# Raw expert projections drawn in the drains of two sixteen-head attentions, and GpSimd's gate products held until the routing is chosen

## The chip, the cores and the metric

One NeuronCore of a Trainium2 chip. The metric is the device time of one execution of the program in microseconds (us), median of several runs. Engines are named as in the profile: PE is TensorE's matmul, PEld its weight load, DVE VectorE, ACT ScalarE, POOL GpSimd, SP the engine that issues DMAs.

## What is computed

A stack of four layers over 16 sequences of 128 tokens of width 128 (2048 tokens in all). Each layer adds a gated cross-attention and a gated feed-forward to the residual stream `x`. The change concerns the last two layers:

```
x = x + tanh(g_xattn[2]) * L2_xattn(layernorm(x), ctx, ctx, mask)      # stage a2, 16 heads of 8
x = x + tanh(g_ffn[2])   * L2_ffn(layernorm(x))                        # stage f2
x = x + tanh(g_xattn[3]) * L3_xattn(layernorm(x), ctx, ctx, mask)      # stage a3, 16 heads of 8
x = x + tanh(g_ffn[3])   * L3_ffn(layernorm(x))                        # stage f3

L2_ffn: p = softmax(x @ gate); keep the top 2 of 8 experts
        y = sum_e p_e * silu(x @ W_e + b_e);  out = y @ combine
L3_ffn: s = sigmoid(x @ gate), 32 experts in 8 groups; best 4 groups, then best 6 experts, renormalised, * 2.5
        y = sum_e c_e * ((silu(x @ g_e) * (x @ u_e)) @ d_e) + one shared expert of the same form
```

## The kernel before

All data stay in SBUF; `x` is held token-major (16 blocks of 128 tokens), `xnt` is the layernormed stream, feature-major. Every stage is one Python function that returns five generator programs, one per engine. `in_turn` strings the stages together on each engine: a program yields twice, and the part ahead of its first yield is placed inside the last part of the stage before it, ahead of what that stage still has to do behind its own second yield. So each engine has one instruction list in a fixed order, with semaphore waits between engines, and nothing is reordered when it runs.

**Attention (`small_head_attention`, a2 and a3).** For each of the 16 blocks, PE makes the scores in banks 0 to 3 of PSUM (L872, L879), DVE takes maxima (L1124) and subtracts them (L1131), ACT takes the exponential (L1049), PE transposes (L893), ACT copies to SBUF (L1072), PE gathers the values (L906), and the result of a block is turned to tokens (L921), normalised on DVE (L1110, L1114), turned back (L930), copied by ACT (L1061), multiplied with `wo` (L937), and added to `x` on DVE (L1100) with its statistics (L1103, L1105). POOL makes the reciprocal roots for pairs of blocks (L325 to L332), ACT scales a pair (L341), PE turns it (L363) and ACT keeps it in `xnt` (L370). The *drain* is what is left after the last block's subtraction: two more blocks' turn-back, `out`, residual, and the last three pairs of blocks. There banks 0 to 3 are free, and PE, ACT and DVE wait for one another in a chain.

**Feed-forward (`feed_forward`, f2 and f3).** The tokens go in NG = 4 groups of 512; with J tiles (experts) there are N = 4 J steps: 32 in f2, 68 in f3. An *up* is the projection of one group with one expert: one 128x512 matmul in f2, a gate (L1788) and a second one (L1781) in f3; in fp32 the profile counts each as two instructions. ACT applies the function and writes to a ring of 512-column slots (L1885); in f3 ACT also copies the second projection (L1891) to one of two slots `u` and POOL multiplies the two (L2019). The routing: `logits` (L1526) for groups 0 to 2 before the first yield and for group 3 after it, a copy by ACT (L1559), a transpose (L1533), then the *choice*, a long chain of small DVE operations (`Route.choose`), then for each group a turn back on PE (L1547, semaphore `parts`) and a copy to `combt` by ACT (L1574). PE's loop over steps m does the up of step m + `ahead`, the selector matmul that spreads the weight of step m (L1809), and the *down* of step m - LAG (L1834; in f2 L1821, for two tiles that POOL has added, L2026). DVE multiplies with the weight (L1965). `ahead` ups are thus done before the choice ends: 12 in f2, 16 in f3. Of these, B = 3 (f2) and 2 (f3) lie ahead of the first yield, so ACT's functions for them stand ahead of its last scale (L341) and keep (L370) of the attention. In f3, from step 8 on, selector weights come by DMA (`spread`) instead of PE.

At the end of a group DVE adds to `x` (L1972) and takes statistics; in f2 POOL makes the root four steps later (L2039 to L2047), ACT scales (L1899) and PE turns (L1844).

`feed_forward` already has `early` and `given`: the first layer's attention a0 lets PE write the first raw projections of f0 (`early_up`) and DVE copy them unchanged from PSUM to the ring (`put_by`, L1799); ACT takes the function in place later (`take_function`). f2, a3 and f3 do without: their `early` is 0.

## Time and profile before

| | us |
|---|---|
| median of 3 runs | 1172.62 (1172.36 to 1173.94) |
| the profiled execution, its own time | 1173.72 |
| its span in the profile | 1172.0 |
| PE busy | 1093.0 (93%) |
| DVE busy | 725.7 (62%) |
| ACT busy | 702.9 (60%) |
| POOL busy | 469.0 (40%) |
| mean granted TensorE clock, share of 2.4 GHz | 0.978 |

The profiled execution is 1.1 us above the median, and 1.7 us of its time lie outside the span. PE is busy nearly everywhere, so what matters is where it is not: the page's forty slices show two tenths of idle PE in the slices of the two drains (slices 27 and 34 of 40, 29.3 us each), and the granted clock below 1 there.

### The profile page before, as it was taken

How to read it: one execution, taken by the hardware profiler on the slowest of the kernel's cores; microseconds unless marked ns; L12 is line 12 of the kernel's file. 1: busy time of each engine (PE TensorE's matmuls, PEld its weight loads, DVE VectorE, ACT ScalarE, POOL GpSimd, SP SyncE). 2: the span in 40 equal slices, each digit the busy share in tenths (PEclk: the TensorE clock that was granted, in tenths of full speed). 3: DMA queues.
4: the chain of work that ended last, by engine and by line, in shares of the span. 5: the costliest groups of instructions: out<-in, count | busy, mean ns of one | idle time of the engine just before them, and what ended most of it. 6: DMA issues, size and time to landing. Idle time of an engine off the chain costs nothing. (4 is left out here: it accounts for less than half of the span.)

```text
span 1172.0 us, 22896 instructions
## 1 busy us (share of the span) xinstructions
PE 1093.0 (93%) x8937; PEld 788.4 (67%) x8937; DVE 725.7 (62%) x1399; ACT 702.9 (60%) x1288; POOL 469.0 (40%) x741
## 2 busy tenths in 40 slices
PE   5998998899999999999997989988979988999998
PEld 3553478788888888888886646653646663466667
DVE  6775666565556656566654259974659994555554
ACT  4674711566665666666665568876458986644440
POOL 5772002223332233443344364431574634544440
PEclk9899999899999999999999999999989998999999
DMA  9200001000000000000000200000000000032220
GB/s 347 83 2 1 1 1 66 8 1 2 1 1 2 1 2 2 1 1 2 1 1 1 55 1 2 2 2 1 1 1 2 1 2 1 10 106 100 99 72 19
DMA packets 13884, 29.42 MB, mean 25 GB/s; under 512 B 2737, under 2 KB 5073, under 8 KB 13010
## 3 DMA queue, kind: packets, MB, share of 16 engines
q1 hardware_dynamic: 13778, 27.96, 6.9%
q8 instruction: 72, 1.18, 0.4%
q14 instruction: 34, 0.28, 0.1%
HBM read 25.14 MB, written 1.25 MB: 23 GB/s over the span
## 5 line engine op out<-in xcount | busy, mean ns | idle before, releaser
L1347 POOL TENSOR_TENSOR work<-work 128x1024 f32<-128x1024 f32 x64 | 121.3, 1896 | 268.2 <-DVE work L1441 268.2
L1428 DVE TENSOR_REDUCE work<-psum 128x8 f32<-128x1024 f32 x64 | 78.0, 1219 | 86.3 <-PE psum L1227 86.3
L1369 ACT ACTIVATE work<-work 128x1024 f32<-128x1024 f32 x64 | 67.4, 1053 | 95.8 <-DVE work L1432 95.8
L1439 DVE TENSOR_REDUCE work<-work 128x8 f32<-128x1024 f32 x64 | 77.4, 1209 | 71.7 <-ACT work L1369 71.7
L1834 PEld LDWEIGHTS psum<-w_down,work 128*128 128x128 f32 x768 | 99.2, 191 | 26.2 <-issue 24.3
L1834 PE MATMUL psum<-w_down,work 128*128 128x128 f32 x768 | 100.6, 275 | 0.9 <-DVE x L1972 0.7
L1124 DVE TENSOR_REDUCE work<-psum 128x8 f32<-128x1024 f32 x64 | 75.4, 1219 | 23.9 <-PE psum L879 23.6
L1072 ACT ACTIVATE work<-psum 128x512 f32<-128x512 f32 x128 | 74.2, 597 | 21.4 <-PE psum L893 20.7
L893 PEld LDWEIGHTS psum<-ident,work 128*128 128x128 f32 x512 | 57.2, 142 | 40.6 <-issue 21.7
L1432 DVE TENSOR_TENSOR work<-psum,work 128x1024 f32<-128x1024 f32 x64 | 78.4, 1225 | 6.7 <-DVE work L1428 0.5
L893 PE MATMUL psum<-ident,work 128*128 128x128 f32 x512 | 76.3, 280 | 5.4 <-ACT work L1072 3.6
L1227 PEld LDWEIGHTS psum<-work 64*128 64x128 f32 x1024 | 59.6, 188 | 24.4 <-issue 23.5
L1131 DVE TENSOR_TENSOR work<-psum,work 128x1024 f32<-128x1024 f32 x64 | 75.0, 1213 | 0.0
L1373 ACT ACTIVATE work<-psum 128x512 f32<-128x512 f32 x128 | 69.1, 596 | 2.3 <-PE psum L1242 2.3
L1242 PE MATMUL psum<-ident,work 128*128 128x128 f32 x512 | 66.4, 273 | 1.3 <-ACT work L1373 1.3
L1049 ACT ACTIVATE work<-work 128x1024 f32<-128x1024 f32 x64 | 67.2, 1053 | 0.2
L1788 PE MATMUL psum<-xnt,ctx_tok 128*128 128x512 f32 x128 | 66.7, 603 | 0.0
L1227 PE MATMUL psum<-work 64*128 64x128 f32 x1024 | 65.8, 278 | 0.7 <-ACT work L1364 0.7
L1781 PE MATMUL psum<-xnt,big 128*128 128x512 f32 x128 | 65.7, 594 | 0.0
L1259 PE MATMUL psum<-work 128*64 128x128 f32 x1024 | 63.0, 276 | 0.0
L1242 PEld LDWEIGHTS psum<-ident,work 128*128 128x128 f32 x512 | 57.9, 141 | 1.7 <-issue 1.7
L2019 POOL TENSOR_TENSOR big<-big,work 128x512 f32<-128x512 f32 x32 | 41.0, 1280 | 44.5 <-ACT work L1891 44.5
(351 smaller groups left out, 2447.5 us busy)
## 6 DMA issues: line engine op xcount, KB each, us to landing
work<-chosen SPq DMA_DIRECT2D x80, 128.0 KB, 3.0
x<-in_x SPq DMA_DIRECT2D x2, 512.0 KB, 4.8
ctx_tok<-in_ctx SPq DMA_DIRECT2D x2, 512.0 KB, 6.3
xnt<-in_xt SPq DMA_DIRECT2D x1, 1024.0 KB, 8.8
ctxt<-in_ctxt SPq DMA_DIRECT2D x1, 1024.0 KB, 10.6
mask<-in_mask SPq DMA_DIRECT2D x1, 1024.0 KB, 9.4
w_down<-in_down SPq DMA_DIRECT2D x1, 1024.0 KB, 7.9
ctx_tok<-in_g SPq DMA_DIRECT2D x1, 1024.0 KB, 4.7
```

What stands on the lines that cost most here:

```text
L893: mm = pe.transpose(bank[4 + g % 2][:, i * P:(i + 1) * P], prob[:, b % 2, h * P:(h + 1) * P], k.ident[:, :])
L1072: act.activation(probt[:, g, :], bank[4 + g % 2][:, :], ACT.Copy).then_inc(S["pt"], 1)
L1124: dve.tensor_reduce(nmax[:, b % 2, 8 * half:8 * half + 8], s, AX.X, ALU.max, negate=True)\
L1131: dve.tensor_tensor(prob[:, b % 2, half * 1024:(half + 1) * 1024] .rearrange("p (h c) -> p h c", c=P), s, nmax[:, b % 2, 8 * half:8 * half ...
L1227: mm = pe.matmul(bank[2 * half + r][:, c * P:(c + 1) * P], qt[rows, u % 2, at:at + P], kt[rows, u % 2, at:at + P], start=True, stop=True)
L1242: mm = pe.transpose(bank[4 + t % 2][:, n * P:(n + 1) * P], prob[:, u % 2, 8 * half + 4 * r + c % 4, :], k.ident[:, :])
L1347: pool.tensor_tensor(prob[:, u % 2, h, :], prob[:, u % 2, h, :], rinv[:, u % 2, h].unsqueeze(2).broadcast_to([P, 8, P]), ALU.mult)\
L1373: act.activation(probt[:, t, :], bank[4 + t % 2][:, :], ACT.Copy).then_inc(S["pt"], 1)
L1428: dve.tensor_reduce(nmax[:, u % 2, h], s, AX.X, ALU.max, negate=True).then_inc(S["max"], 1)
L1432: dve.tensor_tensor(prob[:, u % 2, h, :], s, nmax[:, u % 2, h].unsqueeze(2).broadcast_to([P, 8, P]), ALU.add)\
L1439: dve.tensor_reduce(rsum[:, u % 2, h], prob[:, u % 2, h, :], AX.X, ALU.add).then_inc(S["sum"], 1)
L1834: mm = pe.matmul(y[g % 2][:, b * P:(b + 1) * P], h[:, b * P:(b + 1) * P], tiles[j][4], start=j == 0 and b == 0, stop=j == J - 1, skip_grou ...
```

## The change

Both attentions get the number of the next stage and the number of raw pieces it wants. In the drain PE writes the first three pieces (`early_up`), DVE copies them out between its own steps (`put_by`), and the rest (4 in f2, 5 in f3) come from the next stage's part ahead of its first yield. A piece is one 128x512 projection: f2 takes 7 pieces, which are 7 tiles, f3 takes 8, which are 4 tiles. ACT takes the functions of f3's four tiles at once after the router's scores; f2's seven are spread over its later steps, one per step where f0 had two. `ahead` of f2 goes from 12 to 15, with a longer ring in weights that are no longer needed (wv1, wo1). In f3 the two slots `u` become sixteen, fourteen of them in dead weights, and POOL waits for `parts`, the end of the choice, before its first product. DVE's set-up of a3's key mask, which stood behind f2's choice, now stands ahead of it. Lines of the changed file are 1 to 12 higher than before (L893 is L894, L1788 is L1800, L1885 is L1897, L2019 is L2029).

```diff
@@ small_head_attention, tensor
                 turn(b - 1, 0)
                 if b >= 3:
                     turn_back(b - 3)
+                if b == NB:
+                    pe.wait_ge(S["sub"], 2 * NB)
+                    k.made[next_stage].early_up(pe, 0)
...
+        k.made[next_stage].early_up(pe, 1)
         turn_back(NB - 2)
         out(NB - 2)
         turn_to_tokens(NB - 1)
         after.turn(pe, NB // 2 - 3)
+        k.made[next_stage].early_up(pe, 2)
         turn_back(NB - 1)
@@ small_head_attention, vector
+        k.made[next_stage].put_by(dve, 0)
         residual_of(NB - 3)
         normalise_of(NB - 2)
+        k.made[next_stage].put_by(dve, 1)
         residual_of(NB - 2)
         normalise_of(NB - 1)
+        k.made[next_stage].put_by(dve, 2)
         residual_of(NB - 1)
+        for piece in range(3, pieces):
+            k.made[next_stage].put_by(dve, piece)
@@ feed_forward
-    u = a.take(2 * GT, "p (n c) -> p n c", n=2) if second else None
+    u = [*u_slots, a.take(GT), a.take(GT)] if second else ()
+    U = len(u)
...
-    ring = [one[:, n * GT:(n + 1) * GT] for one in spare for n in range(NG)][:R]
+    ring = [*(one[:, n * GT:(n + 1) * GT] for one in spare for n in range(NG)), *extra][:R]
@@ scalar
-                if n >= early + 2:
-                    act.wait_ge(S["prod"], n - 1)
-                act.activation(u[:, n % 2, :], bank[2 + n % 2][:, :], ACT.Copy).then_inc(S["second"], 1)
+                if n >= U:
+                    act.wait_ge(S["prod"], n - U + 1)
+                act.activation(u[n % U], bank[2 + n % 2][:, :], ACT.Copy).then_inc(S["second"], 1)
...
         for m in range(N + LAG + TURN + 1):
-            for of in (next(functions, None), next(functions, None)):
-                if of is not None:
-                    take_function(of)
             if m + ahead < N:
                 activate(m + ahead)
             if routed and 1 <= m < len(r.turns):
                 r.keep(act, m)
+            if (of := next(functions, None)) is not None:
+                take_function(of)
@@ vector
         yield
+        yield
         if routed:
             r.choose(dve)
         for m in range(N + LAG + TURN + 1):
-            if m == mask_at:
-                yield
@@ gpsimd
         if second:
+            pool.wait_ge(r.S["parts"], 1)
             for n in range(N):
                 multiply(n)
@@ build
-            return feed_forward(k, prev, "f2", 5, up2, ACT.Silu, ahead=12, lags=(4, 7, 8), on_act=True, one_down=True,
-                                spare=(k.big[0], k.big[2], k.negb),
+            return feed_forward(k, prev, "f2", 5, up2, ACT.Silu, ahead=15, lags=(4, 7, 8), on_act=True, one_down=True,
+                                early=7, given=3, extra=halves("wv1", "wo1"), spare=(k.big[0], k.big[2], k.negb),
...
-            return feed_forward(k, prev, "f3", 7, up3, ACT.Silu, ahead=16, lags=(0, 0, 0),
+            return feed_forward(k, prev, "f3", 7, up3, ACT.Silu, ahead=16, lags=(0, 0, 0), early=4, given=3,
+                                u_slots=halves("wq1", "wk1", "wv1", "wo1", "up0", "down0", "wfc", "wproj"),
```

How instructions move. First, PE at the end of a3 before, from the gather of the last block to the last turn of the attention (L363) and f3's first projection (L1788):

```order
L906 MATMUL psum<-work 32x128 x16
L930 MATMUL psum<-ident,work 128x128
L937 MATMUL psum<-w_wo,work 128x128
L921 MATMUL psum<-ident,work 128x128 x2
L363 MATMUL psum<-ident,work 128x128 x2
L930 MATMUL psum<-ident,work 128x128
L937 MATMUL psum<-w_wo,work 128x128
L363 MATMUL psum<-ident,work 128x128 x2
L1526 MATMUL psum<-xnt,w_gate 32x512 x3
L1788 MATMUL psum<-xnt,ctx_tok 128x512
```

and the same place in the changed kernel (numbers are one or a dozen higher):

```order
L907 MATMUL psum<-work 32x128 x16
L1793 MATMUL psum<-xnt,big 128x512
L931 MATMUL psum<-ident,work 128x128
L938 MATMUL psum<-w_wo,work 128x128
L922 MATMUL psum<-ident,work 128x128 x2
L363 MATMUL psum<-ident,work 128x128 x2
L1800 MATMUL psum<-xnt,ctx_tok 128x512
L931 MATMUL psum<-ident,work 128x128
L938 MATMUL psum<-w_wo,work 128x128
L363 MATMUL psum<-ident,work 128x128 x2
L1537 MATMUL psum<-xnt,w_gate 32x512 x3
L1793 MATMUL psum<-xnt,big 128x512
```

Two projections now stand between the drain's small steps (a third, not shown, a little ahead), and five instead of four behind the router's three logits. Second, ACT at the start of f3 before, from its second-last keep (L370) of a3's pairs:

```order
L370 ACTIVATE xnt<-psum 128x256
L1885 ACT_TABLE_LOAD
L1885 ACTIVATE big<-psum 128x512
L1891 ACTIVATE work<-psum 128x512
L1885 ACTIVATE big<-psum 128x512
L1891 ACTIVATE work<-psum 128x512
L341 ACTIVATE work<-x,rstd 128x128 x2
L370 ACTIVATE xnt<-psum 128x256
L1559 ACT_TABLE_LOAD
L1559 ACTIVATE work<-psum 128x512
L1885 ACT_TABLE_LOAD
L1885 ACTIVATE big<-psum 128x512
```

and now:

```order
L370 ACTIVATE xnt<-psum 128x256
L1565 ACT_TABLE_LOAD
L1565 ACTIVATE probe<-floor 128x1
L341 ACTIVATE work<-x,rstd 128x128 x2
L370 ACTIVATE xnt<-psum 128x256
L1570 ACTIVATE work<-psum 128x512
L1918 ACT_TABLE_LOAD
L1918 ACTIVATE big<-big 128x512 x4
L1897 ACTIVATE big<-psum 128x512
L1903 ACTIVATE w_wv<-psum 128x512
```

The last scale of the attention (L341) no longer stands behind two tiles' functions, one of three table loads is gone, and four functions in place (L1918) stand between the scores (L1570) and the first projection that ACT itself evicts. Third, ACT in f2 now, from the scores to the copy of the first group's chosen weights (L1585; before, it stood behind eight functions and two table loads):

```order
L1570 ACTIVATE work<-psum 128x512
L1575 ACTIVATE work<-work 128x128
L1897 ACT_TABLE_LOAD
L1897 ACTIVATE big<-psum,cols 128x512
L1897 ACTIVATE negb<-psum,cols 128x512
L1918 ACTIVATE big<-big,cols 128x512
L1897 ACTIVATE negb<-psum,cols 128x512 x3
L1918 ACTIVATE big<-big,cols 128x512
L1897 ACTIVATE w_wv<-psum,cols 128x512 x2
L1897 ACTIVATE w_wo<-psum,cols 128x512
L1918 ACTIVATE big<-big,cols 128x512
L1585 ACTIVATE combt<-psum 24x512
```

Eleven functions of 512 columns stand ahead of that copy, and the load of the exponential's table (L1575) is gone.

## Rows read from the trace of the kernel before

**Rows 1.** Windows of core 0: from:to, length, busy PE, PEld, DVE, ACT, POOL, clock, DMA

```profile
811.06:814.16 3.10, 3.10 (x12) 1.05 (x12) 2.89 (x9) 2.27 (x5) 0.00 (x0) 1.00 0.00 0
851.00:854.00 3.00, 1.10 (x8) 0.95 (x9) 1.16 (x9) 2.06 (x5) 2.59 (x3) 1.00 0.00 0
967.00:970.00 3.00, 1.26 (x11) 0.83 (x7) 0.76 (x5) 1.25 (x4) 1.72 (x7) 1.00 0.00 0
971.00:977.00 6.00, 5.48 (x14) 2.02 (x14) 0.94 (x5) 2.82 (x5) 2.08 (x8) 0.50 0.01 4
1009.00:1147.00 138.00, 137.75 (x637) 86.52 (x638) 66.24 (x52) 64.92 (x109) 66.09 (x53) 1.00 0.25 82
```

**Rows 2.** Timeline, end of a2: start, us, engine, line, op, [idle before <-releaser]

```profile
799.50 0.44 PE L363 MATMUL psum<-ident,work 128*128 128x128 f32 x2 [1.54 <-ACT work L341]
```

**Rows 3.** Timeline, start of f2

```profile
802.99 0.48 DVE L1620 COPY work<-psum 128x32 f32<-128x32 f32 x4 [10.61 <-PE psum L1533]
...
803.26 1.28 ACT L1564 ACT_TABLE_LOAD   x1
...
804.55 0.31 ACT L1564 ACTIVATE work<-work 128x128 f32<-128x128 f32 x1
...
806.18 1.84 ACT L1885 ACTIVATE big<-psum,cols 128x512 f32<-128x512 f32 x3
...
812.10 0.57 ACT L1574 ACTIVATE combt<-psum 24x512 bf16<-24x512 f32 x1
...
819.88 1.05 PE L1821 MATMUL psum<-w_comb,work 128*128 128x128 f32 x8
...
822.93 1.05 PE L1821 MATMUL psum<-w_comb,work 128*128 128x128 f32 x8
```

**Rows 4.** Timeline, f2 where its ups end

```profile
837.41 0.23 POOL L2039 TENSOR_SCALAR work<-work 128x4 f32<-128x4 f32 x1
...
840.67 1.64 ACT L1899 ACTIVATE work<-x,work 128x128 f32<-128x128 f32 x4
```

**Rows 5.** Timeline, end of a3 and start of f3

```profile
970.66 0.47 PE L930 MATMUL psum<-ident,work 128*128 128x128 f32 x1 [1.38 <-DVE work L1114]
...
981.29 0.44 PE L363 MATMUL psum<-ident,work 128*128 128x128 f32 x2 [1.45 <-ACT work L341]
...
985.64 0.88 DVE L1620 COPY work<-psum 128x128 f32<-128x128 f32 x4 [12.30 <-PE psum L1533]
...
1002.61 1.02 PE L1788 MATMUL psum<-xnt,ctx_tok 128*128 128x512 f32 x2
...
1003.47 1.02 PE L1781 MATMUL psum<-xnt,big 128*128 128x512 f32 x2
...
1009.25 0.42 PE L1547 MATMUL psum<-ident,work 128*96 128x128 bf16 x4 [1.32 <-DVE work L1672]
```

**Rows 6.** DVE's groups by form in f3's choice, 985:1010: busy us, mean ns

```profile
L1637 DVE TENSOR_TENSOR work<-work,rows 128x512 f32<-128x512 f32 x1 | 1.8, 1802 | 0.0
L1670 DVE TENSOR_TENSOR work<-work 128x512 f32<-128x512 f32 x1 | 1.8, 1773 | 0.0
L1669 DVE CAST work<-work 128x512 bf16<-128x512 f32 x1 | 1.4, 1382 | 0.0
L1666 DVE TENSOR_SCALAR work<-work 128x16 f32<-128x16 f32 x1 | 1.2, 1208 | 0.0
L1667 DVE TENSOR_TENSOR work<-work 128x512 f32<-128x512 f32 x1 | 0.7, 692 | 0.0
```

**Rows 7.** The same groups' lines in f0's choice, 112:146, where POOL has no products

```profile
L1669 DVE CAST work<-work 128x256 bf16<-128x256 f32 x1 | 0.3, 293 | 0.0
...
L1666 DVE TENSOR_SCALAR work<-work 128x16 f32<-128x16 f32 x1 | 0.2, 174 | 0.0
```

**Rows 8.** Single lines: ns min/median/max, first and last start

```profile
L1799 DVE COPY big<-psum x8: 658/686/692, 101.4 to 115.7; 128x512 f32<-128x512 f32 x8
...
L2019 POOL TENSOR_TENSOR ctxt<-ctxt,work x12: 1262/1266/1687, 1003.5 to 1110.3; 128x512 f32<-128x512 f32 x12
```

More of the change, by code:

```diff
@@ L800, in small_head_attention @@
 def small_head_attention(k, prev, tag, sub, names, bias_q, bias_k, bv, bo, mask_rows, set_mask, weights_of, selectors,
-                         turn_mask=None):
+                         next_stage, pieces, turn_mask=None):
     nc, bank, psum = k.nc, k.bank, k.psum
@@ L1675, in feed_forward @@
 def feed_forward(k, prev, tag, sub, tiles, function, ahead, lags, one_down=False, routing=None, spare=(), bias=None,
-                 requantise=None, joint=False, on_act=False, head=None, early=0, given=0, raw_second=(), mask_at=0):
+                 requantise=None, joint=False, on_act=False, head=None, early=0, given=0, extra=(), u_slots=()):
     nc, bank = k.nc, k.bank
@@ L1795, in put_by @@
             dve.wait_ge(S["up2"], n + 1)
-            dve.tensor_copy(raw_second[n], bank[2 + n % 2][:, :]).then_inc(S["raw"], 1)
+            dve.tensor_copy(u[n], bank[2 + n % 2][:, :]).then_inc(S["raw"], 1)
         else:
@@ L2018, in multiply @@
                 pool.wait_ge(S["second"], n - early + 1)
-            pool.tensor_tensor(ring[n % R], ring[n % R], raw_second[n] if n < early else u[:, n % 2, :], ALU.mult)\
+            pool.tensor_tensor(ring[n % R], ring[n % R], u[n % U], ALU.mult)\
                 .then_inc(S["prod"], 1)
@@ L2203, in cut, with halves @@
             return w[name][:, n * width:(n + 1) * width]
+        def halves(*names):
+            return [cut(n, at, GT) for n in names for at in range(WEIGHTS[n] // GT)]
         up0 = [(cut("up0", j), None, None, k.sels[:, j * P:(j + 1) * P], cut("down0", j)) for j in range(8)]
@@ L2230, in a2 @@
                                         k.rows[:, R_BV2:R_BV2 + P], k.gated_bo[:, 0, :], k.full_mask_rows,
-                                        k.set_full_mask, 2, (8, 128), k.turn_full_mask)
+                                        k.set_full_mask, 2, (8, 128), 2, 7, k.turn_full_mask)
         def f2(prev):
-            return feed_forward(k, prev, "f2", 5, up2, ACT.Silu, ahead=12, lags=(4, 7, 8), on_act=True, one_down=True,
-                                spare=(k.big[0], k.big[2], k.negb),
+            return feed_forward(k, prev, "f2", 5, up2, ACT.Silu, ahead=15, lags=(4, 7, 8), on_act=True, one_down=True,
+                                early=7, given=3, extra=halves("wv1", "wo1"), spare=(k.big[0], k.big[2], k.negb),
                                 routing=dict(E=8, groups=None, top_groups=None, top=2, kind="softmax",
@@ L2241, in a3 @@
                                         k.rows[:, R_BV3:R_BV3 + P], k.gated_bo[:, 1, :], k.key_mask_rows,
-                                        k.set_key_mask, 3, (32, 64))
+                                        k.set_key_mask, 3, (32, 64), 4, 8)
         def f3(prev):
-            return feed_forward(k, prev, "f3", 7, up3, ACT.Silu, ahead=16, lags=(0, 0, 0),
+            return feed_forward(k, prev, "f3", 7, up3, ACT.Silu, ahead=16, lags=(0, 0, 0), early=4, given=3,
+                                u_slots=halves("wq1", "wk1", "wv1", "wo1", "up0", "down0", "wfc", "wproj"),
                                 spare=(k.big[0], k.big[2], k.negb, k.ctxt),
```

## The prediction

> **What bounds the kernel now.** I read the page's sums first, then the windows around the drains, then the timeline there. PE is busy 93% of the span, so the change can win only where PE waits or runs slowly, and can lose wherever it makes PE wait. In f3's long stretch PE is busy 137.75 of 138 us [rows 1]: there a tile costs what PE's instructions cost, and nothing that DVE, ACT or POOL do shows. That stretch holds 52 steps, so a step is 2.65 us. In the drain of a3 PE is busy 1.26 of 3 us, and behind it the granted clock is 0.50, which is 1.2 GHz instead of 2.4, for 971 to 977 [rows 1]; a2's drain has the same shape. A projection costs 0.86 us at full clock, from start to start of a pair [rows 5], and twice that at 1.2 GHz. Then PE waits again, 1.54 us in f2 [rows 2] and 1.45 us in f3 [rows 5], for ACT's last scale, which stands behind the functions of the tiles drawn ahead. Last, f3's PE waits 1.32 us for the choice, which runs from 985.64 to 1009.2 on DVE [rows 5], 23.6 us, 16 tiles being drawn meanwhile.
>
> **Part 1, the drains.** Three pieces of 0.86 us go into each drain. The first stands in a chain that has no gap (PE to ACT and back), so it delays by 0.86. The second and third stand in gaps that PE has while DVE normalises, of which the third's is 1.38 us [rows 5] and the second's half that, and cost together some 0.2. So the last but one turn comes 1.05 us later. DVE's copies take 0.69 each [rows 8] and fall where DVE waits for PE; their cover is that wait, and without it each would add up to 0.69, 2.1 per drain. Behind that turn come the router's three logits (1.0 at full clock) and four pieces in f2, five in f3: 3.4 and 4.3 us. The attention's last turn follows. It no longer waits for ACT. If the clock stays at its upper level, it starts at 797.5 in a2 (799.50 before [rows 2]) and at about 980.1 in a3 (981.29 before [rows 5]): 2.0 and 1.1 us earlier, although PE has done 7 and 4 tiles rather than 3 and 2.
>
> Whether the clock stays is the unknown. The stretch that now shows PE busy 1.26 of 3 us before the fall gets 1.7 us more work, so it would be busy for about half to three quarters of each such stretch. 851 to 854, with 1.10 of 3, shows the clock at 1.00 throughout [rows 1], so a low share alone doesn't force the fall. I take no fall. A fall costs what seven or eight projections and logits lose at 1.2 GHz until the last turn: 2.7 us in a2, 3.1 in a3.
>
> **Part 2, f2.** Group 3's logits, and all that hangs on them, come 2.0 us earlier, but DVE has the key mask ahead of the choice (3.1 us from 811.06 [rows 1], where it stood behind the choice), ready at 801.4 instead of 802.99 [rows 3]: 1.6 earlier. The exponential's table load, 1.28 [rows 3], disappears from ACT; part of it lay on DVE's path, by my reckoning 0.4. The choice therefore ends near 809.2, 2 us earlier. ACT now decides: behind the exponential (803.0) and one load (804.3) stand eleven functions at 0.61 (1.84 for three [rows 3]), 6.8 us, so the copy of the first chosen weights starts at 811.1 instead of 812.10 [rows 3]. Over the next four steps ACT has four copies and four functions more, but stays ahead of PE. The first down comes at 818.7 instead of 819.88 [rows 3]: **1.2 us gained**, with three more tiles drawn. From there f2 is PE's, 3.04 us for two steps (819.88 to 822.93 [rows 3]), of which an up is 0.86. The three tiles in hand are worth 2.6 us when the ups end, at step 17 instead of 20, if PE is still the bound. It is not: the first group's root on POOL (from 837.41, 3 us) and ACT's scale (1.64 from 840.67 [rows 4]) already gate the turn at step 19, and neither moves. Only DVE's add and statistics of the next group slide under that wait. Bounds 0 and 2.6; I take **1.0**, nearer to what DVE's two microseconds there leave. Sum for f2: 2.2.
>
> **Part 3, f3.** The choice starts when the logits allow: 985.64 less 1.1, 984.5. With POOL silent its slow instructions return to their normal price. L1637 and L1670 (1.80, 1.77 [rows 6]) work on the same sizes as L1667 (0.69): 1.1 each. L1669 (1.38; L1671 repeats it) takes 0.29 for half the size where POOL is quiet [rows 7], so at most 0.59, and some 0.43 with a fixed part: 1.9 for the two. L1666 takes 1.21 against 0.17 [rows 6, 7]: 1.0. That is 5.1 us; the bounds are 0 (if POOL is not the cause) and about 6. The choice then ends at 1002.9, and PE could turn back at 1003.2. PE itself: up 4 and the router's transpose till 984.3; up 5 till 986.0. Up 6 needs ACT's first own eviction. ACT: scores till 983.0, one table load 1.28, four functions in place 2.4, one eviction 0.6: 987.3. PE waits 1.4 us. Then ten tiles of 1.72 (two projections of 0.86 [rows 5]): 1004.6. So PE is later than the choice, by 1.4 us, and the turn back is at 1004.6 instead of 1009.25 [rows 5]: **4.65 us gained**. Behind it every step is PE's as before.
>
> Fourteen products in dead weights cost nothing themselves: sixteen slots replace two, so ACT waits for no product until step 0. The held products are a debt: sixteen at 1.27 us [rows 8] from 1003 on, while PE asks for one per 2.65 us. The debt shrinks by 1.4 us per step and POOL is always ahead of the step that needs it. The cover is 2.65 less 1.27; its slowest product is 1.69 [rows 8].
>
> **The sum.** 2.2 + 4.65 = 6.85 us. The profiled execution goes from 1173.72 to 1166.9; the median, 1.1 lower, from 1172.62 to **1165.8**.
>
> **The rivals.**
> - *The clock falls all the same.* For it: PE still waits for DVE and ACT twice within 3 us at the end of each drain. Against it: 4 us of added work, and the stretch at 851 that didn't fall [rows 1]. Once costs 2.7 or 3.1: 1168.5 to 1168.9. Twice: 1171.6.
> - *The hold doesn't speed up the choice* (DVE's slow instructions have another cause). Then it lasts 23.6 us and ends at 1008.1; f3 gains 0.85 and the time is 1169.6. Against it: f0's choice, without products, shows none of the slow ones [rows 7].
> - *GpSimd becomes the bound, and the kernel slower.* The place: the products behind the choice, in the steps from 8 on, where DVE multiplies two SBUF tensors at the same time as POOL. It decides from 2.6 us per product on, PE's step; at 2.6, 68 of them from 1003 last till 1180, and with some 6 us of weighing, down, add and store the span ends at 1186: 1186.5 for the median. Against it: none is over 1.69 [rows 8].
> - *ACT's table loads cost more than their row.* The trace has the exponential at 804.55, 1.29 us after its load started at 803.26 [rows 3], so a load costs 1.28. If each of the two loads on the path (f2's behind the exponential, f3's behind the scores) took twice that, the gain would be 2.6 less: 1168.4. The Trainium skill (ScalarE: Activation LUTs, What ACT_TABLE_LOAD costs) counts a drain of about 1.38 us behind each load, 2.66 in all; by that figure the sum would be 2.8 us smaller. By that rule, the trace doesn't agree: the next function starts right behind the load.
> - *More is won:* the tail of f2 gives all of its 2.6, and ACT's wait in f3 isn't there: 1.6 + 1.4 more, 1162.8.
>
> **How the numbers follow.** As forecast 50%; one fall of the clock 24%; two 7%; no faster choice 7%; costly loads 2%; more won 6%; GpSimd as bound 2%; something of the drain's cover failing in small, 2%. 0.2% of this kernel, 2.3 us, is about what a measurement can tell from no change, so faster means below 1170.3: all but two falls, GpSimd and the last, 0.88; same 0.09; slower 0.03. The range reaches from the case with more won, 1162.8, to the two falls, 1171.6; I leave out GpSimd's case and half of what lies at either edge.
>
> **What would show it.** Right: the clock at 1.00 through both drains; the last turns (L363) near 797.5 and 980; the five DVE lines of rows 6 at 0.69, 0.43 and 0.17 us, with POOL idle until the choice ends; PE waiting about 1.4 us for ACT at f3's seventh tile; f3's first turn back some 4.65 us earlier measured from a3's last score. Wrong: a clock of 0.50 behind either drain; DVE's chain as slow with POOL idle; PE waiting for products behind step 8; f2's downs no earlier because ACT's functions stand ahead of its first copy.

## The result and the profile after

The changed kernel takes 1170.07 us, median of 8 runs (1167.27 to 1171.33), against 1172.84 (1172.19 to 1174.56, 8 runs) for the kernel before on the same chip: ratio 0.997, 95% interval 0.996 to 0.998, a gain of 2.8 us (2.3 to 4.7). Forecast were 6.85. The profiled execution took 1171.33 us, span 1169.3, against 1173.72 and 1172.0.

First the windows that answer to [rows 1], of the kernel after: from:to, length, busy PE, PEld, DVE, ACT, POOL, clock, DMA. The first two are f2's tail, the next two a3's drain, the last f3's long stretch.

```profile
843.00:846.00 3.00, 3.00 (x14) 2.51 (x14) 1.29 (x2) 0.60 (x1) 0.79 (x2) 0.50 0.00 0
853.00:860.00 7.00, 6.14 (x26) 5.29 (x27) 2.58 (x4) 1.40 (x4) 3.45 (x4) 0.52 0.00 0
971.00:974.00 3.00, 2.63 (x15) 1.36 (x11) 1.28 (x3) 1.25 (x4) 1.71 (x7) 1.00 0.00 0
975.00:982.00 7.00, 6.36 (x21) 2.62 (x22) 3.89 (x8) 3.79 (x8) 2.08 (x8) 1.00 0.01 4
1006.00:1144.00 138.00, 137.62 (x636) 86.01 (x635) 70.07 (x51) 65.42 (x110) 81.49 (x66) 1.00 0.28 82
```

The drain holds its clock at 1.00, where 971 to 977 stood at 0.50 before [rows 1]. But f2's tail, at 1.00 before, now stands at 0.50 in two stretches: 1.2 GHz where PE had 2.4. The last window has 0.38 of idle PE, which I come back to.

The timeline of PE in f2's tail, after: start, us, engine, line, op, [idle before <-releaser]. L1856 is the turn of a finished group, L1821 the selecting matmul, L1833 the down.

```profile
839.36 1.05 PE L1833 MATMUL psum<-w_comb,work 128*128 128x128 f32 x8
842.55 1.08 PE L1856 MATMUL psum<-ident,work 128*128 128x128 f32 x4 [2.15 <-ACT work L1911]
843.42 1.06 PE L1821 MATMUL psum<-combt,sels 128*128 128x512 bf16 x2
844.28 1.91 PE L1833 MATMUL psum<-w_comb,work 128*128 128x128 f32 x8
...
849.41 1.05 PE L1833 MATMUL psum<-w_comb,work 128*128 128x128 f32 x8
853.86 1.11 PE L1856 MATMUL psum<-ident,work 128*128 128x128 f32 x4 [3.40 <-ACT work L1911]
854.76 1.06 PE L1821 MATMUL psum<-combt,sels 128*128 128x512 bf16 x2
855.62 1.91 PE L1833 MATMUL psum<-w_comb,work 128*128 128x128 f32 x8
```

PE idles 2.15 and 3.40 us for ACT's scale. Behind either wait a down takes 1.91 instead of 1.05, two selectors 1.06 instead of 0.59, and DVE, POOL and ACT wait for them. The same two turns in the kernel before:

```profile
842.36 0.66 PE L1844 MATMUL psum<-ident,work 128*128 128x128 f32 x4
...
852.90 0.66 PE L1844 MATMUL psum<-ident,work 128*128 128x128 f32 x4 [3.01 <-ACT work L1899]
853.82 1.05 PE L1821 MATMUL psum<-w_comb,work 128*128 128x128 f32 x8
```

There the first turn had no wait, since the tiles of steps 17 to 19 stood ahead of it. The second waited 3.01 us, and the clock stayed at 1.00 behind it.

The end of a3 and the start of f3 in PE's timeline, after [rows 5]:

```profile
982.08 0.38 PE L363 MATMUL psum<-ident,work 128*128 128x128 f32 x2
982.94 1.05 PE L1537 MATMUL psum<-xnt,w_gate 128*32 128x512 f32 x2 [0.47 <-ACT xnt L370]
...
1005.07 1.02 PE L1793 MATMUL psum<-xnt,big 128*128 128x512 f32 x2
1005.92 0.39 PE L1558 MATMUL psum<-ident,work 128*96 128x128 bf16 x4
```

Neither the last turn nor the turn back waits any more. The slow instructions of f3's choice [rows 6], by form, after:

```profile
L1667 DVE TENSOR_TENSOR work<-work 128x128 f32<-128x128 f32 x4 | 0.9, 286 | 0.0
...
L1681 DVE TENSOR_TENSOR work<-work 128x512 f32<-128x512 f32 x1 | 0.7, 693 | 0.0
L1648 DVE TENSOR_TENSOR work<-work,rows 128x512 f32<-128x512 f32 x1 | 0.7, 691 | 0.0
L1680 DVE CAST work<-work 128x512 bf16<-128x512 f32 x1 | 0.4, 427 | 0.0
L1677 DVE TENSOR_SCALAR work<-work 128x16 f32<-128x16 f32 x1 | 0.2, 175 | 0.0
```

**Where the time went.** One execution starts up to 5 us apart from another: at f0's choice, ahead of everything that the change touches but behind the first loads and a stretch of cold clock, the fourteen profiles of this study lie between 2.3 us earlier and 2.65 us later than the kernel before (the changed kernel is the one 2.65 later). So I compare pieces of the program by starts in each timeline. The marks are: f0's first turn back and first down; in an attention, DVE's first maximum of the last block (L1130); the last L363; f2's first down; its adds (L1983); the fifth block of a3; the first sum of f3's choice (L1648, 0.9 behind its first copy); f3's first turn back (L1558); the last add.

| piece, us | before | after | difference | forecast |
|---|---|---|---|---|
| f0, turn back to first down | 5.29 | 4.71 | -0.58 | 0 |
| a2, last block to last turn | 22.82 | 20.40 | -2.42 | -2.0 |
| last turn to f2's first down | 20.21 | 21.19 | +0.98 | +0.8 |
| first down to f2's 2nd add | 22.38 | 20.12 | -2.26 | -1.0 for these two |
| f2's 2nd to 4th add | 16.74 | 21.44 | +4.70 | together |
| f2's last add to a3's 5th block | 33.00 | 33.32 | +0.32 | 0 |
| a3, last block to start of choice | 28.76 | 26.37 | -2.39 | -1.1 |
| choice to turn back | 22.69 | 18.63 | -4.06 | -3.55 |
| turn back to last add | 158.23 | 158.83 | +0.60 | 0 |

These add up to -5.1. The last add comes only 2.7 us earlier in the changed kernel's profile, because its start came 2.65 later. The medians differ by 2.8, with an interval that reaches to 4.7: of the 4.1 us that are missing from the forecast 6.85, the pieces show 1.7, and 2.3 lie between the pieces of this one pair of profiles and the medians. No profile here says where the other executions of the changed kernel spent those 2.3.

### The profile page after: what moved, and what is told of

It is laid out like the page before. It is cut to its first block and busy times, and to the rows that moved or that the text cites. A ratio compares the mean times of both kernels' runs of the same rounds, so it can differ in the third digit from the quotient of the medians.

```text
span 1169.3 us, 22891 instructions
## 1 busy us (share of the span) xinstructions
PE 1091.3 (93%) x8937; PEld 790.1 (68%) x8937; DVE 734.1 (63%) x1414; ACT 696.1 (60%) x1282; POOL 466.9 (40%) x741
## 5 line engine op out<-in xcount | busy, mean ns | idle before, releaser
L1130 DVE TENSOR_REDUCE work<-psum 128x8 f32<-128x1024 f32 x64 | 75.4, 1220 | 24.0 <-PE psum L880 23.8
L894 PEld LDWEIGHTS psum<-ident,work 128*128 128x128 f32 x512 | 58.0, 143 | 41.1 <-issue 22.7
L894 PE MATMUL psum<-ident,work 128*128 128x128 f32 x512 | 77.0, 282 | 4.6 <-ACT work L1078 3.2
L1800 PE MATMUL psum<-xnt,ctx_tok 128*128 128x512 f32 x128 | 65.7, 595 | 0.6 <-ACT big L1897 0.6
L1976 DVE TENSOR_TENSOR work<-psum,big 128x512 f32<-128x512 f32 x45 | 30.8, 691 | 44.5 <-PE psum L1821 44.3
```

Source lines behind the costliest of these rows:

```text
L894: mm = pe.transpose(bank[4 + g % 2][:, i * P:(i + 1) * P], prob[:, b % 2, h * P:(h + 1) * P], k.ident[:, :])
L1130: dve.tensor_reduce(nmax[:, b % 2, 8 * half:8 * half + 8], s, AX.X, ALU.max, negate=True)\
L1800: pe.matmul(up_banks[n % B][:, :], tiles[j][0], k.xnt[:, tokens], start=True, stop=True)\
```

## The experiments

**Theory A:** with three more tiles drawn ahead, PE has nothing to draw in f2's tail; it idles, the granted clock falls, and the chain there runs on cold matmuls, that is, on matmuls at the lower clock. Rivals: the order of DVE's and POOL's work there; f0 or chance; the early pieces themselves.

**One part at a time.** `f2_only` leaves a3, f3 and the products as before, `f3_only` a2 and f2:

```diff
 f2_only
-    k.set_key_mask, 3, (32, 64), 4, 8)
+    k.set_key_mask, 3, (32, 64), None, 0)          # no pieces
-    f3: early=4, given=3, u_slots=halves(...)
-            pool.wait_ge(r.S["parts"], 1)
 f3_only
-    k.set_full_mask, 2, (8, 128), 2, 7, k.turn_full_mask)
+    k.set_full_mask, 2, (8, 128), None, 0, k.turn_full_mask)
-    f2: ahead=15, early=7, given=3, extra=halves("wv1", "wo1")
+    f2: ahead=12
```

> Only a2 and f2 are changed; a3, f3 and f3's products are as before (f0's and f2's ScalarE order is the changed one). Theory A (f2's tail gives the gain back: without its last three projections PE idles there, the granted clock falls to 0.50 and the selecting and down matmuls on the chain run at 1.2 GHz): the first down of f2 about 1.4 us earlier against a2's last block, the clock at 0.50 near 843 and 853, f2's last add about 1 us later than before, so this part by itself makes the kernel 1 us slower: 1173.8, or 1175.7 if the 1.9 us by which the changed kernel is behind at 780 belong to f0's order and not to chance. The prediction's theory: 2.2 us faster, 1170.6.

> Only a3 and f3 are changed (and the order of ScalarE's functions in f0); a2 and f2 draw as before. Theory A: the turn back of f3 comes 6.5 us earlier, 0.5 are lost again at step 8: 1166.9 (1168.8 if f0's order costs 1.9). The prediction's theory: 4.65 us, 1168.2. In both, f2's tail keeps its clock as in the kernel before, with one fall at its end at most.

`f2_only`: 1173.65 us (11 runs), ratio 1.0003 (0.9994 to 1.0013): the f2 part by itself gains nothing, though f0's 0.58 is in it. Theory A gave 1173.8, the prediction's sum 1170.6. From a2's last block to f2's last add it takes 83.15 us, the changed kernel 83.15, the kernel before 82.16. The windows of its tail show the same clock:

```profile
838.00:841.00 3.00, 3.00 (x14) 2.51 (x14) 1.29 (x2) 0.60 (x1) 0.81 (x2) 0.50 0.03 5
848.00:855.00 7.00, 6.11 (x26) 5.26 (x27) 2.58 (x4) 1.43 (x4) 3.46 (x4) 0.52 0.00 0
```

`f3_only`: 1169.68 (5 runs), 0.9966 (0.9954 to 0.9978). So the gain of the medians comes with the f3 part (and the order of functions in f0, which both runs have). In its profile f2's tail keeps 16.75 us as before; choice to turn back takes 18.63, as in the changed kernel; but a3's drain gives only 0.57 instead of 2.39, since here the clock did fall in it, right behind the last but one turn:

```profile
971.00:975.00 4.00, 2.66 (x14) 1.22 (x15) 2.69 (x9) 1.64 (x5) 0.06 (x2) 1.00 0.01 2
975.00:978.00 3.00, 3.00 (x8) 0.84 (x3) 0.00 (x0) 2.17 (x5) 2.06 (x8) 0.50 0.02 5
```

So a fall in that drain cost 1.8 us here, and it is the larger part of what this run lacks to the 1166.9 that Theory A gave it. With pieces in the drain it is the only fall: a2's drain had none in ten profiles, a3's none in nine of ten; without pieces and without fill the clock fell in every one, three times in either. Start, f0 and chance don't explain f2's loss: it is inside f2, and to 0.02 us the same in two executions that started 4.9 us apart.

**Clock or order.** `f2_warm` puts unread matmuls, whose results nobody uses, into PE's two waits; `f2_ahead12` leaves PE real work there.

```diff
 f2_warm
             if not last_sub and (g := tail_at(m, TURN)) is not None:
+                if one_down and g < 2:
+                    pe.wait_ge(S["act"], N - early)
+                    for _ in range(2 + g):
+                        pe.matmul(bank[0][:, :], tiles[0][0], k.xnt[:, T - GT:T], start=True, stop=True)
                 turn(g)
 f2_ahead12
-    ahead=15, ... early=7, given=3, extra=halves("wv1", "wo1")
+    ahead=12, ... early=7, given=3
```

> The changed kernel, with two matmuls of 128x512 that nobody reads ahead of f2's first turn to PSUM and three ahead of the second, in PE's idle time of 2.15 and 3.40 us. Theory A: the granted clock stays at 1.00 there; turns, selecting and down matmuls behind them take what they take in the kernel before; f2's last add comes 2.4 to 3.4 us earlier: 1167.2. Rival C (order, not clock): no earlier, 1170.1, or later by what the added matmuls delay a turn, at most 0.4 each.

> The changed kernel, with f2 drawing 12 tiles ahead as before and not 15, so that three projections stay in the steps 17 to 19 and PE waits some 2.6 us more for the choice instead. Theory A: the first down is no later, the granted clock stays at 1.00 through f2's tail, and the tail gives back most of its 2.4 us: 1167.3. Rival C (the order of DVE's and GpSimd's work in the tail costs it, not the clock): 1170 as the changed kernel. Prediction's theory (three tiles in hand are worth 1.0): 1171.

`f2_warm`: **1164.44** (6 runs), 0.9932 (0.9920 to 0.9945). PE's timeline of the second wait, where the added matmuls are L1891:

```profile
843.10 1.05 PE L1833 MATMUL psum<-w_comb,work 128*128 128x128 f32 x8
843.99 2.74 PE L1891 MATMUL psum<-xnt,w_ew 128*128 128x512 f32 x6
847.25 0.66 PE L1856 MATMUL psum<-ident,work 128*128 128x128 f32 x4 [0.52 <-ACT work L1915]
847.74 0.59 PE L1821 MATMUL psum<-combt,sels 128*128 128x512 bf16 x2
848.18 1.05 PE L1833 MATMUL psum<-w_comb,work 128*128 128x128 f32 x8
```

The same turn takes 0.66 instead of 1.11, the down 1.05 instead of 1.91. f2's second to fourth add take 17.90 us instead of 21.44, and a2's last block to f2's last add 79.61 instead of 83.15, 3.5 us less where I had expected 2.4 to 3.4. Nothing but PE's five added matmuls differs (and a wait ahead of them until ACT's functions are done), so the order of DVE and POOL is not the cause: the clock is. The 2.55 us that this leaves as the gain over the kernel before is near the 2.2 forecast for f2. (By the two ratios `f2_warm` is 4.5 us faster than the changed kernel, by the pieces of the two profiles 2.6; the rest I can't assign to a place.) In this profile the clock fell at a3's start (858 to 872), and f2's last add to a3's fifth block took 34.28 us, 1.3 more than before. The fill need not be the reason: `f2_only` and `f0_exact`, without it, took 34.23 and 34.24.

```profile
858.00:871.00 13.00, 9.75 (x37) 4.54 (x38) 7.61 (x7) 7.08 (x11) 11.83 (x20) 0.51 0.01 1
```

`f2_ahead12`: 1167.40 (5 runs), 0.9955 (0.9943 to 0.9967). In its profile f2 is no better than the changed kernel's (83.33 us): first down 0.72 later, since PE waited for the choice, its clock fell at 809 and its last draws ran cold; the three ups are back in the steps (22.38); the tail takes 18.64, with one fall instead of two. The first turn has no wait again and no fall. The second waits as long as in the kernel before, behind the same instructions of PE, and yet is cold:

```profile
851.17 1.11 PE L1856 MATMUL psum<-ident,work 128*128 128x128 f32 x4 [3.01 <-ACT work L1911]
852.93 1.91 PE L1833 MATMUL psum<-w_comb,work 128*128 128x128 f32 x8
```

I had expected that the tail gives back most of its 2.4 us, and 1167.3. The time came out, the mechanism did not: by the pieces this kernel is no faster than the changed one, so that agreement is luck. Why a wait of 3.01 us ends cold here and not in the kernel before is open.

**Hold and pieces of f3 apart.** `no_hold` is the changed kernel without POOL's wait; `hold_only` has the wait and the sixteen slots and no pieces.

```diff
 no_hold
-            pool.wait_ge(r.S["parts"], 1)
 hold_only, beside the f3 of the change without early=4, given=3
-    k.set_full_mask, 2, (8, 128), 2, 7, ...   k.set_key_mask, 3, (32, 64), 4, 8)
+    k.set_full_mask, 2, (8, 128), None, 0, ... k.set_key_mask, 3, (32, 64), None, 0)
```

> The changed kernel without the hold: GpSimd's products of the last stage start as soon as ScalarE's values are there, next to the choice. If the hold is what shortens the choice: the choice takes 23.5 us again instead of 17.07 and ends some 4 us behind PE, which waits for it: 1173.6, all of f3's gain gone; the 0.5 us that PE now waits at step 8 for DVE's weighing are back. Rival (the choice's slow instructions have another cause): 1170 as the changed kernel.

> The kernel before with the hold and its sixteen slots alone, no piece in either drain (f0's ScalarE order is the changed one). My theory: the choice ends near 1002.7, but PE then has its sixteen tiles to draw until 1007.9, so the turn back comes only 1.3 us earlier, 0.5 are lost at step 8 and f0 gives 0.6: 1171.5. Rival (the hold alone is worth the whole of the choice's shortening): 6.5 us, 1166.8.

`no_hold`: 1175.15 (12 runs), 1.0017 (1.0005 to 1.0029), slower than the kernel before. `hold_only`: 1171.19 (11 runs), 0.9991 (0.9978 to 1.0004). The choice of `no_hold`, by form, and PE's wait behind it, from its timeline:

```profile
L1667 DVE TENSOR_TENSOR work<-work 128x128 f32<-128x128 f32 x4 | 5.1, 1332 | 0.0
...
L1680 DVE CAST work<-work 128x512 bf16<-128x512 f32 x1 | 1.4, 1369 | 0.0
L1648 DVE TENSOR_TENSOR work<-work,rows 128x512 f32<-128x512 f32 x1 | 1.2, 1170 | 0.0
L1677 DVE TENSOR_SCALAR work<-work 128x16 f32<-128x16 f32 x1 | 1.0, 1012 | 0.0
```

```profile
1009.32 0.66 PE L1558 MATMUL psum<-ident,work 128*96 128x128 bf16 x4 [4.38 <-DVE work L1683]
1009.77 2.02 PE L1800 MATMUL psum<-xnt,w_sg 128*128 128x512 f32 x2
```

From its first copy to its last product the choice takes 24.05 us, against 17.07 with the hold and 23.55 before. PE waits 4.38 us, and behind the wait it is cold (2.02 for what takes 1.02; the clock stands at 0.50 from 1008.7 to 1012.1). The turn back to the last add then takes 159.58 us, 1.35 more than before. `hold_only` has the short choice, 17.07, and gains 1.49 us from its start to the turn back, since PE is still drawing its sixteen tiles. Counted from a3's last block to the turn back, drain and choice together, the hold alone gives 1.5 us, the pieces alone 1.9, both 6.4 (51.44 before, 49.91, 49.54 and 45.00). (`hold_only`'s drains fell to 0.50 as before.) `no_hold` as a whole is slower than the kernel before with f2's cold tail still in it, so its median is not the price of f3's pieces.

**The debt of the held products.** In the changed kernel DVE's timeline at f3's step 8, where weights start to come by DMA and DVE multiplies two SBUF tensors, and POOL's beside it:

```profile
1027.93 0.69 DVE L1976 TENSOR_TENSOR work<-psum,big 128x512 f32<-128x512 f32 x1 [2.13 <-PE psum L1821]
1028.92 7.12 DVE L1976 TENSOR_TENSOR work<-work,negb 128x512 f32<-128x512 f32 x1 [0.30 <-PE psum L1846]
...
1028.08 2.51 POOL L2029 TENSOR_TENSOR big<-big,w_wv 128x512 f32<-128x512 f32 x2
1030.53 2.50 POOL L2029 TENSOR_TENSOR big<-big,w_wo 128x512 f32<-128x512 f32 x2
1032.98 2.51 POOL L2029 TENSOR_TENSOR big<-big,w_up 128x512 f32<-128x512 f32 x2
...
1036.10 1.16 PE L1846 MATMUL psum<-w_down,work 128*128 128x128 f32 x8 [0.38 <-DVE work L1976]
```

One weighing takes 7.12 us: it starts while POOL multiplies without a pause, and ends at 1036.04, 0.55 us after POOL's last product of that burst (1035.49). PE's down at 1036.10 waits 0.38 us for it. The three weighings behind it take 0.68, 1.76 and 0.68. (A wider view of the timeline merges them into one row; the 3.13 us each of my expectation below was the mean of such a row.) In `hold_only` the burst ends at 1030.43 and the same weighing takes 2.12:

```profile
1028.86 2.12 DVE L1976 TENSOR_TENSOR work<-work,negb 128x512 f32<-128x512 f32 x1 [0.30 <-PE psum L1846]
```

There the turn back to the last add takes 158.19 us: nothing is lost, and the 0.5 that I had expected `hold_only` to lose did not come. `paced` makes POOL keep at most six products ahead:

```diff
+            if n >= 8:
+                pool.wait_ge(S["made"], made(n - 6))
             pool.tensor_tensor(ring[n % R], ring[n % R], u[n % U], ALU.mult)\
```

> The changed kernel, with GpSimd's product n from 8 on also waiting until the product n-6 has been weighed, so that the held products are not done in one go. My theory: DVE's weighing of two SBUF tensors took 3.13 us each while GpSimd multiplied without a pause, and PE waited 0.38 us for it at step 8 and ran 0.2 behind; paced, that wait goes and PE's steps in f3 take what they took before: 0.5 us faster, 1169.5. Rival (the waits on the pacing reach PE): later than the changed kernel.

1167.97 (5 runs), 0.9963 (0.9951 to 0.9975). DVE's timeline of `paced` at the same steps:

```profile
1024.96 1.66 DVE L1976 TENSOR_TENSOR work<-work,negb 128x512 f32<-128x512 f32 x1 [0.30 <-PE psum L1846]
1027.58 1.01 DVE L1976 TENSOR_TENSOR work<-work,negb 128x512 f32<-128x512 f32 x1 [0.95 <-PE psum L1846]
1030.19 0.69 DVE L1976 TENSOR_TENSOR work<-work,negb 128x512 f32<-128x512 f32 x1 [1.60 <-PE psum L1846]
```

From the second of these rows on, POOL's products mostly start behind the weighing: 36 of the 40 weighings of two SBUF tensors take 0.69 us, where in the kernel before all 40 were slowed. Turn back to last add takes 158.19 us, as before (158.23), instead of 158.83: the 0.6 is shown by the profile; by the medians, whose intervals overlap, it isn't. One more fall of the clock, in f2's wait for the choice (802.8 to 806.2), made its last turn to first down 22.84 instead of 21.19.

**More fill, and all together.** `warm_more` has `f2_warm`'s five unread matmuls and, in PE's next two waits, two more each: ahead of a3's first score and of f2's last turn. `all_three` adds the pacing.

```diff
         project(0, 2, bank[3])
+        if next_stage == 4:
+            for _ in range(2):
+                pe.matmul(bank[0][:, :], k.w["ew2"][:, 0:P], k.xnt[:, 0:GT], start=True, stop=True)
         pe.wait_ge(S["setup"], 1)
...
+                if one_down and g == 3:
+                    pe.wait_ge(S["added"], NG)
+                    for _ in range(2):
+                        pe.matmul(bank[6][:, :], tiles[0][0], k.xnt[:, T - GT:T], start=True, stop=True)
                 turn(g)
```

> The kernel with two and three unread matmuls ahead of f2's first two turns, and two more of them in each of PE's next two waits: ahead of a3's first score (2.35 us) and ahead of f2's last turn (2.22 us). Theory A: the stretch at 1.2 GHz from 858 to 872 disappears or shrinks; what PE does there on the chain (scores, turns and projections of a3's first block) runs at 2.4 GHz, worth about half of PE's 9 us there if all lay on the chain, and 1 to 3 us as DVE and ACT are on it too: 1162.5. Rival (that stretch is bound by DVE and ACT): 1164.4 as with the first five alone, or later by up to 1.7 where the added ones delay a score.

> The changed kernel with the nine unread matmuls (two and three ahead of f2's first two turns, two ahead of a3's first score, two ahead of f2's last turn) and the paced products. If the parts add: f2's tail and a3's start as with the nine (5.1 us better than the changed kernel from f2's last turn of the attention to a3's fifth block), 0.6 more behind f3's first down. 1163.5; by medians of a few runs its start's chance of some 2 us stands over it. Rival (they don't add, for instance as the clock falls elsewhere): 1165 to 1166.

`warm_more`: 1164.08 (4 runs), 0.9923 (0.9910 to 0.9936). The fall at a3's start shrinks from 858 to 872 to 867.9 to 871.3, and f2's last add to a3's fifth block takes 32.25 us, against 34.28 in `f2_warm`, 33.00 before. The medians don't part the two: their intervals overlap. `all_three`: **1162.53** (6 runs, 1161.36 to 1165.62), 0.9917 (0.9899 to 0.9935): 10 us faster than the kernel before. Its interval overlaps those of `f2_warm` and `warm_more`, so that it is the fastest of the three is shown by the pieces alone. They are those of its parts: 79.59, 32.29 and 158.19, 5.2 us less than in the changed kernel.

**f0.** `f0_order` and `f0_exact` put f0's functions ahead of ACT's own eviction again. The first by my mistake kept one more per step behind it, so its expectation tests less than it says; the second has exactly the order before.

```diff
+            for of in (next(functions, None), next(functions, None)) if sub == 1 else ():
+                if of is not None:
+                    take_function(of)
             if m + ahead < N:
                 activate(m + ahead)
...
-            if (of := next(functions, None)) is not None:
+            if sub > 1 and (of := next(functions, None)) is not None:   # f0_exact; f0_order without sub > 1
```

> The changed kernel with f0's functions again two per step and ahead of ScalarE's own eviction, as before the change; f2 and f3 keep the new order. My theory: in every kernel with the new order f0's first down came 0.57 to 0.60 us earlier against its first turn back than in the kernel before; here those 0.6 us are gone. Rival (they have another cause): they stay.

> The changed kernel with exactly the kernel before's order of ScalarE in f0 (two functions per step ahead of its own eviction, none behind; the run before this one had a third behind). From f0's first turn back to its first down: 5.29 us as in the kernel before, not 4.70 as in the changed one, PE waiting 0.54 us for ScalarE's copy of the chosen weights again. Rival (the 0.59 have another cause): 4.70.

One profile each, 1170.33 and 1168.02 us, which say nothing in single times. From f0's first turn back to its first down `f0_order` takes 5.82, `f0_exact` 5.30, the kernel before 5.29, and all other kernels with the new order 4.71. So the change gains 0.58 in f0: it removes this wait of the kernel before, from PE's timeline.

```profile
138.58 0.38 PE L1547 MATMUL psum<-ident,work 128*48 128x128 bf16 x4 [0.54 <-ACT combt L1574]
```

**Filling the drains without drawing.** `drain_fill` has f2 and f3 as before and an unread matmul in place of each of the three pieces.

```diff
-                    k.made[next_stage].early_up(pe, 0)
+                    pe.matmul(bank[0][:, :], k.w["ew2"][:, 0:P], k.xnt[:, 0:GT], start=True, stop=True)
 (and for pieces 1 and 2; no put_by, early=0 in both stages, f2 ahead=12, no hold)
```

> f2 and f3 as before; in both drains one unread matmul of 128x512 stands where the change has a piece, three per drain. Theory A (busy PE keeps the clock up; the work drawn early matters as well): no fall to 0.50 in the drains or one less, the last but one turn 1.05 us later, the last turn at most 0.5 us earlier, since it waits for ScalarE's scale behind the functions as before: 1172 (f0's order gives 0.6). Rival (the drains' gain is all clock): the last turns 2.0 us earlier as in the changed kernel, 1168.5.

1169.97 (10 runs, 1168.86 to 1174.83), 0.9983 (0.9968 to 0.9998). In its profile the fall of a2's drain comes at 800.5, behind the last turn, and last block to last turn takes 21.30 (22.82 before, 20.40 after); 1.06 is lost again until the first down. In a3's drain the clock falls at 974.6, 4 us later than before and for half as long, and yet the drain gains nothing (29.01): its last turn waits for ACT's scale behind the functions, as before. So this profile shows little gain but f0's, as expected. Yet six of its ten runs are 3.8 to 5.3 us faster than the profiled one (1174.2), and I have no profile of those. This stays open.

## Why the prediction was off

The direction and the range held; the gain was 2.8 us, not 6.85. By the pieces it was 5.1, and even that is a sum of errors of either sign: f2's tail took 3.4 us more than forecast and other places 1.1 more, while f0, the drains and the choice gave 2.8 more. The 2.3 us between pieces and medians stay unexplained. Step by step:

- **Drains, right.** No fall of the clock in the changed kernel's drains, the last but one turn of a2 about 0.9 us later (forecast 1.05), the last turns 2.4 us earlier. I had 2.0 for a2 and only 1.1 for a3. The mechanism was right and the sum was not: from the last but one turn of the kernel before (791.6 and 972.7) the prediction's own terms, 1.05 and then 4.4 or 5.3 us, lead to 797.0 and 979.1, which is 2.5 and 2.2 earlier. That a fall was a matter of chance was right as well: `f3_only` had one. It cost 1.8, not 3.1: the clock was back at 1.00 at 978.4, with half of the instructions up to the turn still to come.
- **f2's start, right.** Copy of the first chosen weights and first down 1.4 us earlier measured from a2's last block (forecast 1.0 and 1.2), with one table load of 1.28 and eleven functions ahead, as laid out.
- **f2's tail, wrong: this is the step that failed.** The prediction took the three tiles in hand for "bounds 0 and 2.6; I take 1.0". It saw that root and scale gate the turns, and concluded that at worst nothing is won. But work that PE loses from a stretch where it waits is not worth zero at worst: PE idled 2.15 and 3.40 us, the clock fell twice, and the tail took 4.70 more against 2.26 won ahead of it: +2.4 instead of -1.0. I had asked about the clock only where the change adds work, the drains, and used 851 to 854 [rows 1], PE busy 1.10 of 3 us with the clock up, as evidence that a low share doesn't force a fall. That reading asked only whether this one stretch was cold, not what the change would take out of the stretches around it. `f2_warm` shows that with the clock held f2 gives 2.55, so the other terms of f2's sum of 2.2 were sound.
- **f3's choice, right in mechanism, undersized.** Choice to turn back gave 4.06 (forecast 3.55), with the drain 6.45 against 4.65. The choice lasts 17.07 instead of 23.55 us, 6.5 less where I had 5.1, beyond my bound of 6. The five lines of [rows 6] and L1671 gave the 5.1 to 0.05 us. The rest is two instructions that I had not read: one of the four small products of 128x128 (L1656 before, L1667 after) took 1.36 and now 0.28, and one `tensor_scalar` (L1664, L1675) 0.41 and now 0.17. PE, not the choice, sets the turn back, as said; its wait for ACT at up 6 was 0.60, not 1.4.
- **The held products, wrong by 0.6.** I costed them against PE's step and found POOL always ahead. It was. Their price lay on DVE, one of whose weighings of two SBUF tensors, at most 1.50 us before, lasted through the whole rest of POOL's burst, 7.12 us, until PE waited for it at step 8. My own rival named this pair of operations, but only from 2.6 us per product on.
- **f0, overlooked.** The order of ACT's functions is shared code; f0 gained 0.58 by it.
- **The rivals.** A fall in a drain did not come in the changed kernel's profile, nor did costly table loads or GpSimd as the bound. "The hold doesn't speed up the choice" is refuted by `no_hold`, 24.05 us against 17.07. Of "more is won" the part in f3 came true for the most part, ACT's wait being 0.60 instead of 1.4, and the part in f2 did not.

## What to carry to other kernels

Before moving work out of a stretch in which TensorE waits, ask what the granted clock does there afterwards, not only whether the moved work was on the path; a few unread matmuls in the waits can be worth nearly as much as the whole change (here nine of them 4.6 us by the pieces of the timelines, the change itself 5.1). Two edits that each remove one of two nearly equal bounds, such as the choice and the drawing beside it, must be costed together: up to f3's turn back the hold alone gave 1.5 us, the pieces alone 1.9, and both 6.4. Held work comes back as a burst. Its price is looked for on every engine that the bursting one slows, and it grows with the length of the burst, not with the mean rate.

## What the hardware showed that I had not expected

- **A wait of 2 to 3 us can end cold or warm.** Without three tiles in f2's tail PE waited 2.15 and 3.40 us in the changed kernel, and the granted clock went from 1.00 to 0.50 behind both, in all six profiles with the tail of the change and no fill. With the tiles it stayed at 1.00, behind a wait of 3.01 us, in the kernel before, `f3_only`, `hold_only` and `drain_fill`; in `f2_ahead12` it fell behind the same 3.01 us. So the length of the wait before it doesn't tell a fall by itself, and what does is open. The Trainium skill (TensorE: Matmul & The Clock Gate, HAM oscillation) describes a matmul kernel in which the waits for DMA between bursts of matmuls put the array back to its lower clock, and advises an order of the loop that keeps it busy. Here the waits are for ScalarE; that the clock stays up when they are filled, the trace agrees: 1.91 to 1.05 us for a down in `f2_warm`.
- **VectorE's product stands while GpSimd's runs.** With two SBUF inputs DVE's 128x512 product takes 0.69 us with POOL silent. In f3's steps each slowed one ended 0.54 or 0.55 us after a product of POOL did, all 40 in the kernel before and all 38 in the changed one. So it takes 1.50 us beside one product per step, 2.12 at the end of `hold_only`'s burst and 7.12 beside products without a pause, which themselves take 1.27 to 1.29. The Trainium skill (SBUF — State Buffer, Who interferes with whom) says that a DVE instruction with two SBUF inputs, and a cast or `tensor_scalar` in a 2-port mode, contends with GpSimd for a shared port. The runs agree on which instructions are slow: L1648 0.69 us against 1.17 to 1.80, L1680 0.43 against 1.37 and 1.38, L1677 0.175 against 1.01 and 1.21.
- **The pieces of a program repeat far better than its start.** Up to f0's choice executions lie 5 us apart. Behind it, pieces in which the clock does the same repeat to a few hundredths: 83.15 us twice, 18.63 nine times. Where it doesn't, equal instructions differ as well: 1.8 us in a3's drain, 1.2 at a3's start, 2.7 between f0's first down and a2's last block. So the table's +0.32 at a3's start may be chance, and small parts were read from pieces and not from medians.
